# Segment attention with unpadded queries, products in quarter and half tiles of the array, and 16 products for the subtraction

## The chip, the cores and the metric

The kernel runs on one core of a Trainium2 chip, in a single launch over a batch of 64 sequences. The metric is the device time of that launch in microseconds (us). The kernel before took 1803.2 us (median of three runs, 1799.8 to 1804.67).

The engines are named as in the profile: PE is TensorE (matrix products, out of PSUM banks 2 KB wide), PEld its loading of the stationary operand, DVE is VectorE, ACT is ScalarE, POOL is GpSimd and SP issues the transfers. They run at once and wait for one another through semaphores.

## The reference, cut to what matters

Every sequence (128 positions, 128 features) goes through a cross-attention block and then this block, of which the change touches the scores and the softmax alone:

```python
xn = rms_norm(x, attn_norm_w)
q, k, v = split(xn @ to_qkv_w)          # 16 heads of 64
q, k = rope(q), rope(k)
kf = concatenate([k_extra, pm, k])      # 16 equal memory keys, 16 persistent keys, 128 own keys
vf = concatenate([v_extra, pm_v, v])
mask = (causal & same_segment) | (ki < 32)   # segments of 64 positions
scores = where(mask, einsum('bhid,bhjd->bhij', q, kf) * 64 ** -0.5, -1e30)
probs = softmax(scores)
o = einsum('bhij,bhjd->bhid', probs, vf)
x = x + o @ to_out_w
x = x + (silu(g) * a) @ ff_w2 + ff_b2        # a, g = halves of rms_norm(x) @ ff_w1 + ff_b1
```

A query sees only the 64 keys of its own segment and the memory keys. The 16 memory keys are equal, so one key with the weight 16 stands for them: 64 + 1 + 16 = 81 keys (`KEYS`) for each segment.

## The kernel before

**Stages and order.** Three sequences are in work at a time. `body(c, a, f)` holds for each engine the instructions of one round: the cross attention of sequence c, the segment attention of sequence a = c - 1 and the output projection and feed-forward of f = c - 2. The 64 sequences give 66 rounds, of which 62 hold all three. The order on each engine is the order of the code, written out by hand; engines meet only in semaphores. PSUM has eight banks: two for the cross attention, four for the segment attention, two for the feed-forward. A helper, `banks`, gives the tasks of a group its banks in turn, and a task may start only when the task before it in its bank has been read.

**The segment attention on PE.** Heads go in pairs, eight pairs of two heads. The transposed queries are copied by ACT into `qpad` (`turned`, L472, two copies of 64 partitions for each half of the pairs). In it the two heads of a pair and one segment form 128 columns; head 0 has its values in partitions 0 to 63 and zeros below, head 1 the other way round, so that one product with the pair's 128 rows of keys gives both heads' scores. Keys are in `kall` by pair and segment, 81 columns each, copied by DVE (L723).

The softmax needs the maximum of each query. It is taken from a first product in bf16 with queries as rows: for each of four tiles `max0` to `max3` one product that adds the causal mask (L979, 256 columns) and four with 81 columns (L982). DVE reduces each tile (L730) and writes the negated maxima as a bf16 pair, high part (L735) and rest (L739), into `mt`; each takes two instructions, for 64 partitions and 64 partitions. The scores proper are a second product in fp32 with keys as rows: 16 products of 128 columns (L872, `scores(t)`), four to a bank. Then PE turns the maxima (L990), ACT copies them into `shift_b`, and 32 products of 64 columns (L880, `less_maxima`) add maxima and mask to the scores. ACT takes the exponentials (L581, `probs`), PE weighs the values (L888, `weigh`), DVE divides (L675, L676, into `o`), and PE turns the result in the next round (L898).

**What stands around it.** In the same round PE does the cross attention's scores and its weighing (L854), which waits for ACT's exponentials (L523), which wait for DVE's clamping (L658). After L854 come the maxima (L979, L982), the scores (L872), L996 (the output projection of the cross attention, which waits for DVE's `c0T`, L668), L880, L1005 (the end of the feed-forward) and L888. The next round begins with L905, the transpose of `xn`: it waits for `xn` (DVE, L785) and for the bank that `pv1` had, which DVE frees with the second L676. DVE's order is: clamp, key copies (L723), a reciprocal (L662), the four maxima (L730), `mt`, a second reciprocal, `c0T`, `sT` (L752), the layer norm `r`, `bn`, `y` (L758 to L770) with a step on POOL in it (L464), then L675 and L676 with `xn` between. ACT's order is: the four L523, the second `turned`, the values `vall` (L472), `shift_b`, four `probs`. The fourth tile of the maxima waits for `vall`, as it takes the bank of the values.

## Time and profile before

| | |
|---|---|
| median of three runs | 1803.2 us |
| lowest and highest | 1799.8, 1804.67 us |
| span of the profiled execution, first to last instruction | 1801.7 us |
| mean granted TensorE clock | 0.997 of full speed |
| PE, PEld, DVE busy | 1666.4, 1434.9, 1543.8 us |
| ACT, POOL busy | 1073.9, 856.9 us |
| transfers from HBM | 21.46 MB read, 14 GB/s over the span with the writes |

The page gives no time for the profiled execution but its span. PE's records overlap, since a matmul's record reaches from its start to the end of its results; a busy PE is therefore not PE at its limit, and the distance from one start to the next is the figure to read. A product in fp32 leaves two records, each with its own load of weights; one in bf16 leaves one.

### The profile page before, as it was taken

What the parts mean: (1) busy time and instruction counts of PE and PEld (TensorE: products, weight loads), DVE (VectorE), ACT (ScalarE), POOL (GpSimd) and SP (SyncE); (2) the same over time, 40 slices, a digit from 0 to 9 for tenths busy, and PEclk for the clock granted to TensorE, in tenths of its full rate; (3) what the DMA queues carried; (4) which work ended last, traced back from release to release, by engine and by line L of the source; (5) the groups of instructions that cost most, each with busy time, mean ns of one, the idle gap of its engine ahead of it and who ended that gap; (6) DMA issues with size and microseconds to landing.
All of it is one profiled execution on the core that took longest, in us unless ns stands there. A gap on an engine that the chain in (4) does not pass through costs nothing.

```text
span 1801.7 us, 52360 instructions
## 1 busy us (share of the span) xinstructions
PE 1666.4 (92%) x17891; PEld 1434.9 (80%) x17891; DVE 1543.8 (86%) x3730; ACT 1073.9 (60%) x2637; POOL 856.9 (48%) x1107
## 2 busy tenths in 40 slices
PE   4899999999999999999999999999999999999997
PEld 3788788788888887888888888887888888878876
DVE  5788888889889889888888888888888898898894
ACT  3555656655656656656556556566566556566563
POOL 4344534535535535445445445445355355355352
PEclk9999999999999999999999999999999999999999
DMA  6000000000000000000000000000000000000000
GB/s 176 17 9 11 10 10 11 8 13 11 8 13 11 8 13 11 8 11 12 8 11 13 8 11 13 8 11 8 12 11 8 13 11 8 13 11 8 13 6 6
DMA packets 32411, 26.14 MB, mean 15 GB/s; under 512 B 8118, under 2 KB 31179, under 8 KB 32139
## 3 DMA queue, kind: packets, MB, share of 16 engines
q1 hardware_dynamic: 32394, 25.93, 5.4%
q8 instruction: 9, 0.15, 0.0%
q14 instruction: 8, 0.06, 0.0%
HBM read 21.46 MB, written 4.46 MB: 14 GB/s over the span
## 4 chain that ended last, share of the span: by engine, by line
DVE 49%; PE 22%; issue 21%; ACT 3%; POOL 3%; DVEq 1%; DMA 1%; SPq 0%; ACTq 0%; POOLq 0%
DVE z L658 9%; PE psum L927 6%; DVE ra L641 5%; DVE z L650 5%; DVE rb L644 5%; DVE mx L730 4%; PE psum L854 4%; DVE rden L662 3%; PE psum L898 3%; DVE sT L752 3%; DVE o L676 3%; DVE c0T L668 2%; ACT z L523 2%; POOL st L464 2%; DVE y L770 1%
## 5 line engine op out<-in xcount | busy, mean ns | idle before, releaser
L409 POOL TENSOR_TENSOR ra<-ra,rb 128x512 f32<-128x512 f32 x256 | 332.2, 1324 | 0.2
L464 POOL TENSOR_TENSOR st<-st,nhalf 128x1 f32<-128x1 f32 x64 | 38.3, 598 | 535.4 <-DVE st L763 535.4
L872 PE MATMUL psum<-qpad,kall 128*81 128x128 f32 x2048 | 251.6, 276 | 0.0
L641 DVE TENSOR_TENSOR ra<-psum,rope 128x512 f32<-128x512 f32 x256 | 174.3, 681 | 77.9 <-PE psum L838 77.8
L872 PEld LDWEIGHTS psum<-qpad,kall 128*81 128x81 f32 x2048 | 224.9, 151 | 2.6
L658 DVE TENSOR_SCALAR z<-z 77x512 f32<-77x512 f32 x256 | 216.8, 885 | 0.0
L581 ACT ACTIVATE probs<-psum 81x512 f32<-81x512 f32 x256 | 131.3, 593 | 142.3 <-PE psum L880 142.3
L523 ACT ACTIVATE z<-z 77x512 f32<-77x512 f32 x256 | 154.1, 627 | 67.1 <-DVE z L658 65.5
L854 PE MATMUL psum<-z,v 77*64 77x128 f32 x2048 | 141.6, 280 | 44.9 <-ACT z L523 44.9
L644 DVE TENSOR_TENSOR rb<-psum,rope 128x512 f32<-128x512 f32 x256 | 173.0, 676 | 0.0
L836 PE MATMUL psum<-wqkv_hi,xnT_hi 128*128 128x512 f32 x384 | 168.6, 439 | 2.7 <-DVE xnT_lo L681 1.8
L854 PEld LDWEIGHTS psum<-z,v 77*64 77x64 f32 x2048 | 112.5, 138 | 69.6 <-issue 68.6
L650 DVE TENSOR_TENSOR z<-psum,wT 77x512 f32<-77x512 f32 x256 | 163.1, 674 | 4.8 <-PE psum L846 4.8
L418 POOL TENSOR_TENSOR q0T_rest<-q0T,q0T_hi 128x128 f32<-128x128 f32 x64 | 29.3, 457 | 288.9 <-ACT k0T_hi L537 288.9
L472 ACT ACTIVATE qpad<-psum 64x512 f32<-64x512 f32 x256 | 151.9, 593 | 3.1
L472 ACT ACTIVATE vall<-psum 64x512 f32<-64x512 f32 x256 | 151.2, 591 | 3.1
L838 PE MATMUL psum<-wqkv_hi,xnT_lo 128*128 128x512 f32 x384 | 152.9, 398 | 0.0
L837 PE MATMUL psum<-wqkv_lo,xnT_hi 128*128 128x512 f32 x384 | 152.4, 397 | 0.0
L863 PE MATMUL psum<-cross_w,ra 128*128 128x128 f32 x1024 | 143.2, 273 | 0.1
L863 PEld LDWEIGHTS psum<-cross_w,ra 128*128 128x128 f32 x1024 | 122.2, 141 | 20.7 <-ACT vall L472 0.4
L888 PE MATMUL psum<-vall,probs 81*64 81x65 f32 x4096 | 133.6, 223 | 0.3 <-ACT probs L581 0.3
L888 PEld LDWEIGHTS psum<-vall,probs 81*64 81x64 f32 x4096 | 124.8, 137 | 8.0 <-issue 0.4
(141 smaller groups left out, 4028.3 us busy)
## 6 DMA issues: line engine op xcount, KB each, us to landing
seq_in<-in SPq DMA_DIRECT2D x64, 166.5 KB
out<-out_sb SPq DMA_DIRECT2D x64, 64.0 KB, 1.6
maskT<-in SPq DMA_DIRECT2D x64, 38.5 KB
vall<-memv_dram SPq DMA_DIRECT2D x128, 4.0 KB, 1.9
ctx_all<-in SPq DMA_DIRECT2D x5, 320.0 KB, 12.3
wqkv<-in SPq DMA_DIRECT2D x1, 1536.0 KB, 10.1
stage<-in SPq DMA_DIRECT2D x1, 1296.0 KB
ctx_all<-in SPq DMA_DIRECT2D x3, 288.0 KB, 11.3
```

Source lines behind the costliest of these rows:

```text
L409: nc.gpsimd.tensor_tensor(ra[:, sl], ra[:, sl], rb[:, sl], ALU.add).then_inc(rot_ready, 1)
L472: copy = lambda out, in_, **k: nc.scalar.activation(out, in_, ACT.Copy, **k)
L523: nc.scalar.activation(zt, zt, ACT.Exp, scale=float(HD0) ** -0.5).then_inc(exp0_ready, 1)
L641: V.tensor_tensor(ra[:, sl].rearrange("n (h d) -> n h d", h=8), p, rope[:, 0, :].unsqueeze(1).broadcast_to([S, 8, DH]), ALU.mult)
L644: V.tensor_tensor(rb[:, sl].rearrange("n (h e t) -> n h e t", h=8, t=2), p, rope[:, 1, :].rearrange("n (e t) -> n e t", t=2).unsqueeze(1). ...
L650: V.tensor_tensor(z0[:, 4 * t:4 * t + 4, :], cross_at(f"score{t}")[0:S2, :].rearrange("k (h q) -> k h q", h=4), wT[:].unsqueeze(1).broadca ...
L658: V.tensor_scalar(zt, zt, lim, -lim, ALU.min, ALU.max).then_inc(clip_ready, 1)
L836: mm(self_at(name), xnT_hi[:], wqkv_hi[:, w], stop=False)
L854: last = mm(cross_at(f"pv{t}")[half:half + 64, 0:S], v0_flat[:, lo:lo + 64], z0[:, 4 * g + r, :], start=r == 0, stop=r == 3)
L863: last = nc.tensor.transpose(self_at(f"{name}T")[:, 128 * n:128 * (n + 1)], ra[:, lo + 128 * n:lo + 128 * (n + 1)], ident[:])
L872: mm(self_at(f"score{t}")[0:KEYS, 128 * n:128 * (n + 1)], kall[:, pair, s, :], qpad[:, pair, s, :, :].rearrange("p h i -> p (h i)"), start ...
L888: last = mm(self_at(f"pv{t}")[SEG * s:SEG * (s + 1), VW * n:VW * (n + 1)], probs[:, pair, s, h, :], vall[s][:, w:w + VW])
```

## The change

Queries lose their zeros: `qT` holds each pair's 128 rows by 128 positions, and one ACT copy of 128 partitions takes the place of two of 64. Since a head's queries and keys lie in one half of the partitions, products run on half of the array's rows: head 0 of a pair in rows 0 to 63, head 1 in rows 64 to 127, each into a bank of its own. The tiles `t` now hold four heads of one parity in place of two pairs; a step works on two banks at a time (`maxima(half)`, `scores(half)`).

- Maxima: per half two mask products, then 16 products of 64 rows, 64 queries and 81 keys. Queries of segment 0 go to partitions 0 to 63 and of segment 1 to 64 to 127, so each product uses a quarter of the array.
- Negated maxima: `mt` has 128 partitions and 16 columns for each part; two DVE instructions in place of four.
- Scores: 32 fp32 products of 64 rows, 81 keys and 64 queries in place of 16 with 128 rows and 128 columns.
- Subtraction: 16 products of 128 columns in place of 32 of 64. The selecting table is half as large.
- The turned maxima go to the unused last 128 columns of the feed-forward's `gate` bank, with a semaphore of their own, and no longer through a bank of the segment attention.
- `o` is written with a stride of two heads; `turn_heads(t)` waits for two tiles at once.

```diff
-        qpad = sb("qpad", [128, PAIRS, NSEG, 2, SEG])
+        qT = sb("qT", [128, PAIRS, S])
...
-                    for h in range(2):
-                        rows = slice(DH * h, DH * (h + 1))
-                        last = copy(qpad[rows, 4 * t:4 * t + 4, :, h, :],
-                                    self_at(f"q{t}T")[rows, :].rearrange("p (c s i) -> p c s i", c=4, s=NSEG))
-                    last.then_inc(q_ready, 1)
+                    copy(qT[:, 4 * t:4 * t + 4, :].rearrange("p c i -> p (c i)"), self_at(f"q{t}T")).then_inc(q_ready, 1)
...
+                    then(V.tensor_scalar(mt[:, 0, :], mx[:], -1.0, None, ALU.mult), self_steps, "hi", a)
+                    V.scalar_tensor_tensor(out=mt[:, 1, :], in0=mx[:], scalar=-1.0, in1=mt[:, 0, :],
+                                           op0=ALU.mult, op1=ALU.subtract).then_inc(mt_ready, 1)
...
+                def maxima(half):
+                    if half == 1:
+                        wait(pe, self_free("max3", a))
+                    for t in (2 * half, 2 * half + 1):
+                        p = self_at(f"max{t}")[:, 0:4 * KEYS].rearrange("i (n k) -> i n k", n=4)
+                        mm(p[:, :, 0:SEG], ident_b[:], causal_b[:].unsqueeze(1).broadcast_to([128, 4, SEG]), stop=False)
                     for n in range(4):
+                        for h in range(2):
+                            t, dims = 2 * half + h, slice(DH * h, DH * (h + 1))
+                            for s in range(NSEG):
+                                queries = slice(SEG * s, SEG * (s + 1))
+                                last = mm(self_at(f"max{t}")[queries, KEYS * n:KEYS * (n + 1)], q_upper[dims, 4 * half + n, queries],
+                                          k_upper[dims, 4 * half + n, s, :], start=False)
+                            if n == 3:
+                                last.then_inc(self_fill(f"max{t}"), 1)
+
+                def scores(half):
+                    wait(pe, self_free(f"score{2 * half + 1}", a))
+                    for n in range(4):
+                        for s in range(NSEG):
+                            for h in range(2):
+                                t, dims = 2 * half + h, slice(DH * h, DH * (h + 1))
+                                mm(self_at(f"score{t}")[0:KEYS, S * n + SEG * s:S * n + SEG * (s + 1)], kall[dims, 4 * half + n, s, :],
+                                   qT[dims, 4 * half + n, SEG * s:SEG * (s + 1)], start=n == 0 and s == 0, stop=False)
 
                 def less_maxima(t):
                     for n in range(4):
-                        pair, s = 2 * t + n // 2, n % 2
-                        p = self_at(f"score{t}")[0:KEYS, 128 * n:128 * (n + 1)]
-                        for h in range(2):
-                            last = mm(p[:, SEG * h:SEG * (h + 1)], select_b[:, (2 * pair + h) * NSEG + s, :], shift_b[:], start=False)
+                        last = mm(self_at(f"score{t}")[0:KEYS, S * n:S * (n + 1)], select_b[:, 4 * t + n, :], shift_b[:], start=False)
...
+                    maxima(0)
+                    maxima(1)
                     scores(0)
+                    if f is not None:
+                        pe.wait_ge(gate_ready, f + 1)
+                    pe.wait_ge(mt_ready, a + 1)
+                    mm(shift_at[0:2 * H, :], mt[:].rearrange("i p h -> i (p h)"), ident_b[:]).then_inc(shift_filled, 1)
                     scores(1)
```

PE before, in the loop, from the cross attention's weighing (`z,v`) to the turned maxima (`stack_b,mt`); in brackets the semaphores waited for:

```order
L854 MATMUL psum<-z,v 64x128 x7
L972 REGISTER_ALU
L979 MATMUL psum<-causal_b,ident_b 128x4x64 [waits memk_ready,k_ready,q_ready]
L982 MATMUL psum<-kall,qpad 128x81 x4
L979 MATMUL psum<-causal_b,ident_b 128x4x64
L982 MATMUL psum<-kall,qpad 128x81 x4
...
L979 MATMUL psum<-causal_b,ident_b 128x4x64 [waits v_ready]
L982 MATMUL psum<-kall,qpad 128x81 x4
L872 MATMUL psum<-qpad,kall 81x128 [waits max_ready]
L872 MATMUL psum<-qpad,kall 81x128 x3
...
L990 MATMUL psum<-stack_b,mt 64x64 [waits mt_ready,max_ready]
```

The same stretch of PE in the changed kernel, to `cross_w,c0T` (L996 before):

```order
L844 MATMUL psum<-z,v 64x128 x7
L974 REGISTER_ALU
L862 MATMUL psum<-causal_b,ident_b 128x4x64 [waits memk_ready,k_ready,q_ready]
L862 MATMUL psum<-causal_b,ident_b 128x4x64
L868 MATMUL psum<-kall,qT 64x81 x16
L862 MATMUL psum<-causal_b,ident_b 128x4x64 [waits v_ready]
...
L879 MATMUL psum<-qT,kall 81x64 [waits max_ready]
L879 MATMUL psum<-qT,kall 81x64 x15
L983 MATMUL psum<-ident_b,mt 32x128 [waits mt_ready,gate_ready]
...
L987 REGISTER_ALU [waits shift_ready]
L988 MATMUL psum<-cross_w,c0T 128x128 [waits c0T_ready]
```

The first tile of the maxima was complete after one mask product and four others, and is now complete after two mask products and 14 small ones. The wait for `v_ready` stood before the fourth tile and stands now before the third and fourth.

DVE before, from the third and fourth maxima to the second reciprocal:

```order
L730 TENSOR_REDUCE mx<-psum 128x4 [waits self_bank4_filled]
L732 ISA
L735 TENSOR_SCALAR mt<-mx 64x16 [waits max_ready]
L735 TENSOR_SCALAR mt<-mx 64x16
L99 REGISTER_ALU
L739 SCALAR_TENSOR_TENSOR mt<-mx,mt 64x16 [waits self_step]
L739 SCALAR_TENSOR_TENSOR mt<-mx,mt 64x16
```

and in the changed kernel:

```order
L726 TENSOR_REDUCE mx<-psum 128x4 [waits self_bank4_filled]
L728 ISA
L729 TENSOR_SCALAR mt<-mx 128x16 [waits max_ready]
L99 REGISTER_ALU
L730 SCALAR_TENSOR_TENSOR mt<-mx,mt 128x16 [waits self_step]
```

Two of the four instructions are gone; the wait of the second part for the first has stayed.

## Rows read from the trace of the kernel before

**Rows 1.** The page: engines' busy time; shares of the chain that ended last.
```profile
PE 1666.4 (92%) x17891; PEld 1434.9 (80%) x17891; DVE 1543.8 (86%) x3730; ACT 1073.9 (60%) x2637; POOL 856.9 (48%) x1107
DVE 49%; PE 22%; issue 21%; ACT 3%; POOL 3%; DVEq 1%; DMA 1%; SPq 0%; ACTq 0%; POOLq 0%
```

**Rows 2.** The chain of waits, two rounds: start us, us, what.
```profile
906.25 1.09 PE psum L854 x16
...
910.39 0.97 DVE rden L662
...
917.72 0.32 PE psum L905
...
944.97 0.32 PE psum L905
```

**Rows 3.** The timeline of DVE: start us, us, what [idle before <-releaser].
```profile
907.87 1.72 DVE L730 TENSOR_REDUCE mx<-psum 128x4 f32<-128x324 f32 x4 [0.36 <-PE psum L982]
909.62 0.35 DVE L735 TENSOR_SCALAR mt<-mx 64x16 bf16<-64x16 f32 x2
911.38 1.20 DVE L668 TENSOR_TENSOR c0T<-psum,rden 32x128 f32<-32x128 f32 x4
912.61 0.86 DVE L752 SCALAR_TENSOR_TENSOR sT<-psum,cols,ug 128x128 f32<-128x128 f32 x3
...
908.68 0.90 DVE L730 TENSOR_REDUCE mx<-psum 128x4 f32<-128x324 f32 x2
```

**Rows 4.** Waits over the whole span: total us, times, longest.
```profile
PE psum L905 <- DVE o L676: 36.5, 63, 0.7
```

**Rows 5.** The timeline of PE in the same round.
```profile
907.50 0.33 PE L982 MATMUL psum<-kall,qpad 128*128 128x81 bf16 x4
908.60 0.29 PE L979 MATMUL psum<-causal_b,ident_b 128*128 128x256 bf16 x1 [0.23 <-ACT vall L472]
908.89 1.94 PE L872 MATMUL psum<-qpad,kall 128*81 128x128 f32 x16
910.76 0.22 PE L990 MATMUL psum<-stack_b,mt 128*64 128x64 bf16 x1
...
912.72 0.40 PE L996 MATMUL psum<-cross_w,c0T 128*128 128x128 f32 x2
912.95 1.42 PE L880 MATMUL psum<-shift_b,select_b 128*81 128x64 bf16 x32
...
915.05 2.09 PE L888 MATMUL psum<-vall,probs 81*64 81x65 f32 x64
```

**Rows 6.** Groups of PE instructions, shapes apart: count, busy us, mean ns.
```profile
L872 PE MATMUL psum<-qpad,kall 128*81 128x128 f32 x2048 | 251.6, 276 | 0.0
L854 PE MATMUL psum<-z,v 77*64 77x128 f32 x2048 | 141.6, 280 | 44.9 <-ACT z L523 44.9
L888 PE MATMUL psum<-vall,probs 81*64 81x65 f32 x4096 | 133.6, 223 | 0.3 <-ACT probs L581 0.3
L880 PE MATMUL psum<-shift_b,select_b 128*81 128x64 bf16 x2048 | 90.8, 203 | 0.0
```

**Rows 7.** The timeline of PE, the last two transposes before L854, and L854.
```profile
904.17 0.38 PE L863 MATMUL psum<-cross_w,ra 128*128 128x128 f32 x2
...
904.48 1.09 PE L854 MATMUL psum<-z,v 77*64 77x128 f32 x16
```

**Rows 8.** The timeline of ACT in the same round; one group of ACT (mean ns).
```profile
906.13 1.20 ACT L472 ACTIVATE qpad<-psum 64x512 f32<-64x512 f32 x2
907.35 1.20 ACT L472 ACTIVATE vall<-psum 64x512 f32<-64x512 f32 x2
...
L472 ACT ACTIVATE oT<-psum 128x512 f32<-128x512 f32 x128 | 76.6, 599 | 36.2 <-PE psum L898 31.4
```

**Rows 9.** First round with segment attention (DVE), and the last one (PE).
```profile
66.35 0.29 DVE L758 TENSOR_TENSOR r<-psum,xb 128x128 f32<-128x128 f32 x1 [0.58 <-PE psum L996]
...
1777.11 1.94 PE L872 MATMUL psum<-qpad,kall 128*81 128x128 f32 x16
```

More of the change, by code:

```diff
@@ L146, in build @@
         causal_b = sb("causal_b", [128, SEG], BF16)
-        select_b = sb("select_b", [128, H * NSEG, KEYS], BF16)
-        stack_b = sb("stack_b", [128, SEG], BF16)
-        shift_b = sb("shift_b", [128, SEG], BF16)
+        select_b = sb("select_b", [128, H, KEYS], BF16)
+        shift_b = sb("shift_b", [128, S], BF16)
         seq_in = sb("seq_in", [128, S + S2 + D])
@@ L392, in _ @@
             nc.gpsimd.memset(nhalf[:], -0.5).then_inc(nhalf_set, 1)
-            for t in (v0, *vall, qpad, mt, half_gate, tanh_gate):
+            for t in (v0, *vall, half_gate, tanh_gate):
                 nc.gpsimd.memset(t[:], 0.0).then_inc(zeros_step, 1)
-            pool.wait_ge(zeros_step, 7)
+            pool.wait_ge(zeros_step, 5)
             nc.gpsimd.memset(v0[:, :, :, 4 * HD0:5 * HD0], 1.0).then_inc(zeros_set, 1)
@@ L576, in body @@
                     values(1)
-                    wait(act, self_filled("shift", a))
-                    copy(shift_b[0:64, :], self_at("shift")[0:64, 0:SEG]).then_inc(shift_ready, 1)
+                    act.wait_ge(shift_filled, a + 1)
+                    copy(shift_b[0:2 * H, :], shift_at[0:2 * H, :]).then_inc(shift_ready, 1)
                     for t in range(4):
                         wait(act, self_filled(f"score{t}", a))
-                        nc.scalar.activation(probs[:, 2 * t:2 * t + 2, :, :, :].rearrange("k c s h i -> k (c s h i)"),
+                        nc.scalar.activation(probs[:, 4 * t:4 * t + 4, :].rearrange("k n i -> k (n i)"),
                                              self_at(f"score{t}")[0:KEYS, :], ACT.Exp, scale=float(DH) ** -0.5).then_inc(probs_ready, 1)
@@ L732, in body @@
                     dve.wait_ge(max_ready, a * 4 + 4)
-                    for h in range(2):
-                        rows = slice(SEG * h, SEG * (h + 1))
-                        last = V.tensor_scalar(mt[rows, h, 0, :], mx[rows, :], -1.0, None, ALU.mult)
-                    then(last, self_steps, "hi", a)
-                    for h in range(2):
-                        rows = slice(SEG * h, SEG * (h + 1))
-                        last = V.scalar_tensor_tensor(out=mt[rows, h, 1, :], in0=mx[rows, :], scalar=-1.0, in1=mt[rows, h, 0, :],
-                                                      op0=ALU.mult, op1=ALU.subtract)
-                    last.then_inc(mt_ready, 1)
+                    then(V.tensor_scalar(mt[:, 0, :], mx[:], -1.0, None, ALU.mult), self_steps, "hi", a)
+                    V.scalar_tensor_tensor(out=mt[:, 1, :], in0=mx[:], scalar=-1.0, in1=mt[:, 0, :],
+                                           op0=ALU.mult, op1=ALU.subtract).then_inc(mt_ready, 1)
                 if c is not None:
@@ L1032, in constants @@
     i = np.arange(SEG)
+    stack = np.tile(np.eye(SEG), (2, 1)).astype(f)
     causal = np.tile(np.where(i[None, :] > i[:, None], NEG, 0.0), (2, 1)).astype(f)
-    stack = np.tile(np.eye(SEG), (2, 1)).astype(f)
-    shift = np.concatenate([np.zeros((64, SEG)), np.where(i[:, None] > i[None, :], NEG, 0.0)]).astype(f)
-    select = np.zeros((128, H, NSEG, KEYS), f)
-    for s in range(NSEG):
-        for part in range(2):
-            for h in range(H):
-                select[h % 2 * 32 + part * 16 + h // 2 * NSEG + s, h, s, :] = 1.0
+    shift = np.tile(np.concatenate([np.zeros((64, SEG)), np.where(i[:, None] > i[None, :], NEG, 0.0)]), (1, NSEG)).astype(f)
+    select = np.zeros((128, H, KEYS), f)
+    for part in range(2):
+        for h in range(H):
+            select[part * H + h, h, :] = 1.0
     for j in range(SEG):
-        select[64 + j, :, :, j] = 1.0
+        select[64 + j, :, j] = 1.0
     return {"ident": np.eye(128, dtype=f), "headmask": headmask, "rope": rope,
```

57 lines of the change are left out of this document (17 added, 40 removed).

## The prediction

> **What bounds the kernel now.** I read the engines' busy time first. PE stands at 92% and DVE at 86% [rows 1], and that alone doesn't say which of them to relieve. The shares of the chain that ended last do: DVE holds 49% of it, PE 22% [rows 1]. So I followed the chain of waits through one round. From the start of L905 at 917.72 to the next at 944.97 it is 27.25 us [rows 2], and 62 rounds of this form make up most of the span. In it PE has the chain in two places. One is the stretch from L905 to the output projection, which the change leaves alone. The other is L854, from 906.25, and behind it the first tile of the maxima [rows 2], which the change rewrites. From the first L730 on, at 907.87 after an idle time of 0.36 us on DVE [rows 3], the chain is DVE's, but for a step on POOL, until L905. There it is PE that waits: for `o` of DVE, 63 times, 36.5 us in all, 0.58 us a round [rows 4].
>
> The reader is to see in this that most of what PE saves behind the maxima, the scores and the subtraction, lies beside DVE's chain. It makes PE's wait at L905 longer and the round no shorter. What counts is when the four maxima are reduced, and how long `mt` takes. I therefore work out one moment: the start of the second reciprocal L662, at 910.39 before [rows 2].
>
> **Spacing of products.** Records overlap, so I take the distance between starts: length of a series less one record, over the number of gaps. Full array, fp32, 128 columns (L872): (1.94 - 0.276)/15 = 0.111 us a record [rows 5, 6]. Half the array's columns, fp32, 128 columns, two halves in turn (L854): (1.09 - 0.28)/15 = 0.054 [rows 6, 7]. Same columns, half the distance: two column halves do run at once. With 65 columns (L888) it is (2.09 - 0.223)/63 = 0.030 [rows 5, 6]. In bf16 on the full array, 64 columns (L880) take (1.42 - 0.203)/31 = 0.039 and 81 columns (L982) (0.33 - 0.20)/3 = 0.042 [rows 5, 6].
>
> **Change of tile form.** The last transpose L863 starts at 904.17 + 0.38 - 0.27 = 904.28; the next start is due 0.111 later, at 904.39, and L854, on half the columns, starts at 904.48 [rows 7]: 0.09 late. The same at L990, narrower than what stands around it: due at 908.89 + 16 x 0.111 = 910.67, started at 910.76 [rows 5], 0.09 again. Each change of form costs 0.09. The Trainium skill (TensorEngine Tiling (Array Packing), Key Properties) says that changing the tiling mode, not just the tile, drains TensorE; the trace agrees with its 0.09 us. It speaks against this change, which alternates between full and quarter tiles.
>
> **ACT's copies.** `turned` costs 1.20 us from 906.13 [rows 8] and becomes one copy of 128 partitions by the same 512 columns: 0.60, as each of the two now takes, since a copy of 128 partitions (`oT`, 599 ns [rows 8]) takes no longer than one of 64. So `q_ready` comes at 906.73 in place of 907.33, and `vall` ends at 907.95 in place of 908.55. The last L854 starts at 906.25 + 1.09 - 0.28 = 907.07 [rows 2, 6]; the next start is due at 907.13 and, after a change of form, at 907.22. Before, L979 came at 907.38, 0.12 ahead of L982 at 907.50 [rows 5]. Gain here: 0.16. What is late next is PE itself.
>
> **Maxima, first half.** Two L979 take 2 x 0.12 = 0.24, then 0.09 for the form: the first small product starts at 907.55. The last one of tile 0 is the fourteenth, 13 distances on. No row shows products on half of the rows, so the distance X is bounded: from above 0.042 us (L982, nothing overlaps), from below 0.042/4 = 0.010 (all four quarters at once). I take 0.030, the shortest that any row has (L888), and it is from products that overlap in just this manner; by columns alone two at once would need 0.021, but L880 shows by 0.039 for 64 columns that small products don't shrink with their columns. Tile 0 then has its last start at 907.94. Before, the last L982 started at 907.50 + 0.33 - 0.20 = 907.63 and L730 at 907.87, 0.24 later. Now L730: 908.18, later by 0.31.
>
> **Second half.** PE is free at 907.55 + 16 x 0.030 = 908.03 and with a change of form at 908.12, after `vall` (907.95, and 0.05 to wake PE, as 908.55 to 908.60 before [rows 5, 8]). So the wait that moved ahead of two tiles costs nothing here. Then 0.24 + 0.09 + 0.39 + 0.24: tile 2 can be reduced at 909.08. DVE would be there at 908.18 + 0.81 (the third L730 stood at 908.68, 0.81 behind the first [rows 3]) = 908.99, so it waits 0.09. From the third L730 to `mt` it was 909.62 - 908.68 = 0.94 [rows 3]: now 910.02, later by 0.40.
>
> **`mt`.** Before 910.39 - 909.62 = 0.77. The second of each two costs about 0.18 (0.35 for two [rows 3], one 0.17). Two such go: 0.41 stay. L662 starts at 910.43, against 910.39: +0.04, or +0.03 with L888's unrounded 0.0297. Over 62 rounds +2 us.
>
> **The rest of PE.** Scores: 64 records in place of 32. With 64 columns and half of the rows I bound them by 0.030 (L888) and 0.057 (half of L872's 0.111, nothing overlaps), and take 0.039, since the 81 columns of weights are those of L880. That is 2.5 us in place of 3.6. Subtraction: 16 x about 0.058 = 0.9 in place of 32 x 0.039 = 1.25. All of it is covered: the second half of the scores ends near 911.9, L996 must wait for `c0T` (911.38 + 1.20 = 912.58 [rows 3]), and DVE needs L996 only after `sT`, at 913.39 or so. Even at 0.057 the scores end near 913.0 and L996 near 913.4, as DVE asks for it. Behind the new wait for `mt_ready` and `gate_ready` stands the second half of the scores, for which nobody waits before that; `gate_ready` is from several microseconds before. The turned maxima's own bank, the smaller `shift_b`, the coarser wait in `turn_heads` (L905 waits for the same second tile already) and the stride of `o` I cost at nothing, covered by the same wait of PE at L905 (0.58).
>
> **Ends.** In the first round with segment attention DVE waits 0.58 for L996 [rows 9] and `mt` is quicker: about -0.7. In the last round nothing of cross attention stands beside PE, which runs unbroken from 1777.11 [rows 9]; scores and subtraction count there, less the slower maxima and the wait for `mt`: about -0.9. The smaller table and the zeros no longer set lie beside loads in the setup.
>
> **Sum.** Span 1801.7 + 2 - 1.6 = 1802.1 us. The page gives no time around the span; the median of the runs stands 1.5 above it, inside their own spread, and I add it: 1803.6. What can be told from no change is 0.3%, 5.4 us.
>
> **Rivals.**
> Quarters overlap further (X at most 0.025). For it speaks that L854 shows full overlap of two halves, and that four quarters can be distinct here; against it that no row is under 0.030. At 0.025: L730 at 907.55 + 0.33 + 0.24 = 908.12, tile 2 at 908.94, `mt` at 909.88, L662 at 910.29, -0.10 a round: -6.5 - 1.6, that is 1795. At 0.010 the second half waits for `vall` at 908.00 and reduces at 908.70, so DVE binds: L730 at 907.92, L662 at 910.08, -0.31 a round: 1782. The Trainium skill gives such a floor (TensorEngine Tiling (Array Packing), Instruction Overhead): a matmul has about 60 cycles of overhead, so that one column takes as long as 60. By that rule X would be an estimated 0.025, this rival's 1795; no run here shows it yet.
>
> Half of the rows don't overlap (slower). X is that of the bf16 products on the full array, 0.0395. For it: rows in halves appear nowhere in the trace, and L880 and L982 are both near 0.04. L730 comes at 908.30, tile 2 at 907.55 + 0.63 + 0.09 + 0.24 + 0.09 + 0.51 + 0.24 = 909.35, L662 at 910.70: +0.32 a round, +20 - 1.6: 1821. It decides from X = 0.033 on: L662 moves by 29 X - 0.83, which is then 0.12 a round.
>
> PE becomes the bound: a load of weights into a half of the rows can't overlap with that half's product, the scores' distance is 0.030 + 0.057 = 0.087, 2.8 us for each half. From 909.1 on they end at 914.9 with the turned maxima between, L996 ends 2.0 us after DVE asks for it, and a round is 2.0 longer: 1925. Against it: L888 alternates in the same manner and shows none of this.
>
> **Chances.** Forecast 0.44, its own range 1799 to 1809 (X from 0.027 to 0.033). More overlap 0.29, no overlap 0.23, PE as the bound 0.04. A tenth of the forecast falls below -0.3% and as much above +0.3%. Faster: 0.29 less a twentieth, and 0.05: 0.33. Slower: 0.23 + 0.04 + 0.04: 0.31. Same: 0.36. The range takes in 0.010 us on one side and 0.042 on the other: 1781 to 1824.
>
> **What would show it.** The distance between starts in the small products of the maxima, 0.030; L730's first start 1.93 us behind that of the last L854 group (before 1.62), its idle time 0.6 to 0.7 in place of 0.36; 0.41 from the first `mt` to L662; idle time of PE at L905 about 1.2 and a new one of some 0.6 before L996, with the round at 27.28. A round shorter by 0.1 or more, or an idle time of DVE before the third L730 over 0.3, would make the prediction wrong.

## The result, and the profile after

The changed kernel takes 1790.68 us (median of four runs, 1787.09 to 1794.01) against 1801.85 for the kernel before, measured beside it (four runs, 1799.8 to 1804.67). The ratio is 0.9933 with an interval of 0.9913 to 0.9952: faster by 0.7%. No change was forecast, so the forecast was wrong; the rival "Quarters overlap further" had the mechanism. Ratios, here and below, are those on record, taken only over executions within 1.5% of the fastest of their kernel (this leaves out one of e7); they are not the quotient of the two medians.

| profiled execution | before | after |
|---|---|---|
| its time, us | not given | 1787.09 |
| span, us | 1801.7 | 1785.3 |
| mean granted TensorE clock | 0.997 | 0.995 |
| 62 full rounds, start to start of the transpose of `xn` | 55 of about 27.24, 6 of 27.54, 1 of 28.48 | 29 of about 26.87, 32 of 27.17, 1 of 29.93 |
| before the second transpose of `xn`; from the last one to the end | 70.64; 39.33 | 69.00; 37.87 |

The spans differ by 16.4 us. The base round, the shortest common one, is 0.37 shorter, 62 x 0.37 = 22.9 us gained. 26 more rounds are 0.30 longer (+7.8), the one round in which the clock falls costs 3.06 in place of 1.24 (+1.8), and the two ends are 1.6 and 1.5 shorter. -22.9 + 7.8 + 1.8 - 3.1 = -16.4.

The page after, against [rows 1]: busy time, and the shares of the chain that ended last.

```profile
PE 1579.7 (88%) x19939; PEld 1321.2 (74%) x19939; DVE 1524.4 (85%) x3601; ACT 985.5 (55%) x2509; POOL 852.2 (48%) x1105
DVE 50%; PE 23%; issue 20%; POOL 3%; ACT 3%; DVEq 1%; DMA 1%; SPq 0%; ACTq 0%; POOLq 0%
```

PE has lost 87 us of busy time and the chain is DVE's as before. The waits over the whole span (total us, times, longest), against [rows 4]:

```profile
PE psum L907 <- DVE o L672: 60.0, 63, 1.0
PE psum L988 <- DVE c0T L664: 32.0, 63, 2.3
```

PE waits 23.5 us more at the start of a round, and there is a new wait for `c0T`: what PE saved behind the maxima turned into waiting, as was argued. A third wait was in no forecast: before the scores PE now waits for DVE to read the first maxima, 23.5 us in all (L879 below). The gain has to be in front of the second reciprocal. PE's timeline in a round with the clock at 1.00 (start us, us, what), against [rows 5, 7]:

```profile
922.77 1.09 PE L844 MATMUL psum<-z,v 77*64 77x128 f32 x16 [1.01 <-ACT z L520]
923.79 0.40 PE L862 MATMUL psum<-causal_b,ident_b 128*128 128x256 bf16 x2
924.12 0.35 PE L868 MATMUL psum<-kall,qT 64*64 64x81 bf16 x16
924.41 0.40 PE L862 MATMUL psum<-causal_b,ident_b 128*128 128x256 bf16 x2
924.73 0.35 PE L868 MATMUL psum<-kall,qT 64*64 64x81 bf16 x16
925.46 1.38 PE L879 MATMUL psum<-qT,kall 64*81 64x64 f32 x32 [0.38 <-DVE mx L726]
...
928.78 0.49 PE L988 MATMUL psum<-cross_w,c0T 128*128 128x128 f32 x2 [0.48 <-DVE c0T L664]
929.10 1.06 PE L884 MATMUL psum<-shift_b,select_b 128*81 128x128 bf16 x16
...
933.87 0.32 PE L907 MATMUL psum<-cross_w,xn 128*128 128x128 f32 x1 [0.97 <-DVE o L672]
```

and the groups that give one record's length (busy us, mean ns), against [rows 6]:

```profile
L879 PE MATMUL psum<-qT,kall 64*81 64x64 f32 x4096 | 178.2, 237 | 23.6 <-DVE mx L726 23.5
L868 PE MATMUL psum<-kall,qT 64*64 64x81 bf16 x2048 | 45.7, 209 | 0.0
```

The distance between starts of the small maxima products is (0.35 - 0.209)/15 = 0.009 us, not 0.030. (The timeline merges records; by the starts of the single ones it is 0.155/15 = 0.010.) That of the scores is (1.38 - 0.237)/31 = 0.037; I had taken 0.039. DVE's timeline in the same round, against [rows 2, 3]:

```profile
924.51 1.70 DVE L726 TENSOR_REDUCE mx<-psum 128x4 f32<-128x324 f32 x4 [0.49 <-PE psum L868]
926.24 0.17 DVE L729 TENSOR_SCALAR mt<-mx 128x16 bf16<-128x16 f32 x1
926.45 0.17 DVE L730 SCALAR_TENSOR_TENSOR mt<-mx,mt 128x16 bf16<-128x16 f32 x1
926.54 0.95 DVE L658 RECIPROCAL rden<-psum 128x128 f32<-128x128 f32 x1
```

The four maxima run on without a gap, and the second reciprocal starts 3.77 us behind the start of L844. Before it was 910.39 - 906.25 = 4.14 [rows 2]. The difference is the 0.37 of the base round. Its parts, before and after: from the start of the weighing to the first maximum 1.62 and 1.74, from there to `mt` 1.75 and 1.73, from `mt` to the reciprocal 0.77 and 0.30. Against the kernel before, the gain is thus all in `mt`.

The longer rounds come from DVE's clamps. Here are the clamps of the second pair and POOL beside them, first in a base round and then in a long one:

```profile
893.22 1.29 POOL L446 TENSOR_TENSOR ug<-ug,half_gate 128x384 f32<-128x384 f32 x1
893.24 1.55 DVE L654 TENSOR_SCALAR z<-z 77x512 f32<-77x512 f32 x2
...
920.09 0.99 POOL L446 TENSOR_TENSOR ug<-ug,half_gate 128x384 f32<-128x384 f32 x1
920.11 1.85 DVE L654 TENSOR_SCALAR z<-z 77x512 f32<-77x512 f32 x2
```

The pair takes 1.55 or 1.85 us, and when it takes 1.55 it is POOL's multiplication that is lengthened, 1.29 in place of 0.99. Both kernels have both forms, and in these two traces the changed one has the dear one more often. Whether the two engines hold each other up there is what e2 tests.

### The profile page after: what moved, and what is told of

It is laid out like the page before. It is cut to its first block, busy times and chain, and to the rows that moved or that the text cites. A ratio compares the mean times of both kernels' runs of the same rounds, so it can differ in the third digit from the quotient of the medians.

```text
span 1785.3 us, 55646 instructions
## 1 busy us (share of the span) xinstructions
PE 1579.7 (88%) x19939; PEld 1321.2 (74%) x19939; DVE 1524.4 (85%) x3601; ACT 985.5 (55%) x2509; POOL 852.2 (48%) x1105
## 4 chain that ended last, share of the span: by engine, by line
DVE 50%; PE 23%; issue 20%; POOL 3%; ACT 3%; DVEq 1%; DMA 1%; SPq 0%; ACTq 0%; POOLq 0%
DVE z L654 8%; PE psum L929 6%; DVE ra L637 5%; DVE z L646 5%; DVE rb L640 5%; DVE mx L726 4%; PE psum L844 4%; DVE rden L658 3%; PE psum L900 3%; DVE sT L742 3%; DVE o L672 3%; DVE c0T L664 2%; ACT z L520 2%; POOL st L465 2%; DVE x1sq L688 2%
## 5 line engine op out<-in xcount | busy, mean ns | idle before, releaser
L410 POOL TENSOR_TENSOR ra<-ra,rb 128x512 f32<-128x512 f32 x256 | 332.3, 1328 | 0.2
L654 DVE TENSOR_SCALAR z<-z 77x512 f32<-77x512 f32 x256 | 225.5, 919 | 0.0
L520 ACT ACTIVATE z<-z 77x512 f32<-77x512 f32 x256 | 161.1, 636 | 114.6 <-DVE z L654 108.1
L879 PE MATMUL psum<-qT,kall 64*81 64x64 f32 x4096 | 178.2, 237 | 23.6 <-DVE mx L726 23.5
L844 PE MATMUL psum<-z,v 77*64 77x128 f32 x2048 | 141.5, 280 | 55.3 <-ACT z L520 55.3
L879 PEld LDWEIGHTS psum<-qT,kall 64*81 64x81 f32 x4096 | 160.4, 150 | 36.2 <-DVE mx L726 31.9
L844 PEld LDWEIGHTS psum<-z,v 77*64 77x64 f32 x2048 | 112.5, 138 | 80.1 <-issue 78.1
L726 DVE TENSOR_REDUCE mx<-psum 128x4 f32<-128x324 f32 x256 | 108.8, 487 | 31.9 <-PE psum L868 31.8
```

Source lines behind the costliest of these rows:

```text
L410: nc.gpsimd.tensor_tensor(ra[:, sl], ra[:, sl], rb[:, sl], ALU.add).then_inc(rot_ready, 1)
L520: nc.scalar.activation(zt, zt, ACT.Exp, scale=float(HD0) ** -0.5).then_inc(exp0_ready, 1)
L654: V.tensor_scalar(zt, zt, lim, -lim, ALU.min, ALU.max).then_inc(clip_ready, 1)
L726: V.reduce_max(mx[:, 4 * t:4 * t + 4], self_at(f"max{t}")[:, 0:4 * KEYS].rearrange("i (n k) -> i n k", n=4), AX_X).then_inc(max_ready, 1)
L844: last = mm(cross_at(f"pv{t}")[half:half + 64, 0:S], v0_flat[:, lo:lo + 64], z0[:, 4 * g + r, :], start=r == 0, stop=r == 3)
L879: mm(self_at(f"score{t}")[0:KEYS, S * n + SEG * s:S * n + SEG * (s + 1)], kall[dims, 4 * half + n, s, :], qT[dims, 4 * half + n, SEG * s:S ...
```

## The experiments

Each kernel is the changed one with the edit shown, unless another is named. "Base round" is the shortest common distance between two transposes of `xn`. The kernel before, run beside them, had medians of 1800.75, 1803.78 and 1801.74 in the three groups of runs (e1 to e4, e5 to e8, e9 to e11).

**e1: `mt` in four instructions.**

```diff
-                    then(V.tensor_scalar(mt[:, 0, :], mx[:], -1.0, None, ALU.mult), self_steps, "hi", a)
+                    for h in range(2):
+                        rows = slice(SEG * h, SEG * (h + 1))
+                        last = V.tensor_scalar(mt[rows, 0, :], mx[rows, :], -1.0, None, ALU.mult)
+                    then(last, self_steps, "hi", a)
...
```

> The changed kernel with the negated maxima again in two instructions of 64 partitions for each part, four in all. If the fewer instructions for mt are what shortens a round, then from the first mt instruction to the second reciprocal it is 0.77 us again in place of 0.30, a round has 27.34 us in place of 26.87, and 62 rounds cost 29 us: about 1820 us. The forecast's own figure for this step was 0.36 us a round: about 1813 us. Rival: the gain comes from the products and the copies alone; then the time stays at 1791 us, within 5.

Measured: 1817.68 (1813.21 to 1827.9), ratio to before 1.0079 (1.0052 to 1.0107). DVE's timeline:

```profile
923.12 0.35 DVE L731 TENSOR_SCALAR mt<-mx 64x16 bf16<-64x16 f32 x2
923.51 0.35 DVE L735 SCALAR_TENSOR_TENSOR mt<-mx,mt 64x16 bf16<-64x16 f32 x2
923.90 0.96 DVE L658 RECIPROCAL rden<-psum 128x128 f32<-128x128 f32 x1
```

From `mt` to the reciprocal it is 0.78, against 0.30 with two instructions, and the base round is 27.35, 0.48 longer. Two tiny instructions are worth their full 0.24 us each on this chain.

**e2: POOL's multiplications of `ug` held back until the last clamp.**

```diff
+                    if c is not None:
+                        pool.wait_ge(clip_ready, c * 4 + 4)
```

> The changed kernel, in which POOL starts its two products for the feed-forward's gate (ug) only when DVE has done the last of the four clamps (one more wait on POOL, in rounds with cross attention). Theory: the rounds of 27.17 us beside those of 26.87 come from the third and fourth clamp (SBUF to SBUF, one source) running at the same time as POOL's ug, and DVE and POOL can't both use what they share: whichever comes second stands still. Then the pair of clamps takes about 0.75 us in place of 1.55 or 1.85, all rounds get one length near 26.1 us, and the time is 1735 to 1745 us. Rival: the long rounds come from something else (ACT's exponentials beside the clamps, PE's clock); then both lengths stay and the time stays within 10 us of 1791, or gets longer because ug is late for DVE's sT.

Measured: 1739.53 (1737.56 to 1740.78), ratio 0.9656 (0.9638 to 0.9674). DVE and POOL:

```profile
923.62 0.75 DVE L656 TENSOR_SCALAR z<-z 77x512 f32<-77x512 f32 x2
...
924.45 1.00 POOL L446 TENSOR_TENSOR ug<-tanh_gate,half_gate 128x384 f32<-128x384 f32 x1 [1.88 <-DVE z L656]
```

(This L446 is the first multiplication, with `tanh_gate`, which stands in L444 of the changed kernel.) The pair takes 0.75, 61 of the 62 rounds are 26.24 to 26.28 long (one 26.17), and no round has a fall of the clock. So the two engines do hold each other up, and both the 0.30 of the long rounds and another 0.6 of every round came from it. The first pair of clamps still takes 1.85 in every round here, beside POOL's `ra` (L410); that one was not held back in any run. The Trainium skill (SBUF — State Buffer, Who interferes with whom) states that VectorE in a two-port mode and GpSimd share a port pair, one of them waiting for the whole instruction of the other. The runs agree: 0.75 alone, 1.55 or 1.85 beside POOL. They don't show the port itself, and the order of the starts doesn't tell who gets it: in all 62 rounds of the changed kernel POOL's multiplication starts first. Where the clamp follows 0.012 to 0.024 us behind, the first clamp runs undisturbed (0.41) and the second takes 1.22; where it follows 0.022 to 0.025 behind, the first takes 1.26 and POOL is not lengthened.

**e3: the small maxima products four in a row on one quarter** (head outermost, then segment, then pair).

```diff
-                    for n in range(4):
-                        for h in range(2):
-                            t, dims = 2 * half + h, slice(DH * h, DH * (h + 1))
-                            for s in range(NSEG):
+                    for h in range(2):
+                        t, dims = 2 * half + h, slice(DH * h, DH * (h + 1))
+                        for s, n in [(s, n) for s in range(NSEG) for n in range(4)]:
...
```

> The changed kernel with the 16 small products of a half in another order: four in a row use the same quarter of the array (first the head, then the segment, then the pair), so that no two neighbours lie in different quarters except at three places. If the distance of 0.009 us between them comes from four quarters at work at once, it grows to 0.035 to 0.042 us, the first tile of the maxima comes about 0.15 us later, the third one 0.5 us later, and a round is about 0.3 us longer: 1805 to 1812 us. If the small products are quick for another reason (64 rows, no drain between them), the distance stays near 0.01 and the time at 1791 us.

Measured: 1783.46 (1780.43 to 1788.14), ratio 0.9906 (0.9883 to 0.993). PE's timeline:

```profile
921.84 0.38 PE L867 MATMUL psum<-kall,qT 64*64 64x81 bf16 x16
```

The distance is (0.38 - 0.209)/15 = 0.011, the base round 26.90. The time is below that of the changed kernel since 11 rounds are long and not 32, and none has a fall of the clock. My expectation missed: products need not take turns among quarters to overlap, at least with four in a row. That left two readings, which e7 tells apart.

**e4: the queries turned in two copies of 64 partitions.**

```diff
-                    copy(qT[:, 4 * t:4 * t + 4, :].rearrange("p c i -> p (c i)"), self_at(f"q{t}T")).then_inc(q_ready, 1)
+                    for h in range(2):
+                        rows = slice(DH * h, DH * (h + 1))
+                        last = copy(qT[rows, 4 * t:4 * t + 4, :].rearrange("p c i -> p (c i)"), self_at(f"q{t}T")[rows, :])
+                    last.then_inc(q_ready, 1)
```

> The changed kernel with ACT's copy of the turned queries in two instructions of 64 partitions each, as before. By the timeline the values (vall) then end 0.6 us later, and with them the second half of the maxima starts about 0.4 us later, so that DVE waits 0.2 us before the third maxima: a round of 27.07 us in place of 26.87, +12 us, 1803 us. If ACT's copy is covered by PE and DVE (rival), the time stays at 1791 us. How many rounds have the longer pair of clamps may change too, as ACT's instructions move; a theory in which only DVE and POOL decide it expects about half of them again.

Measured: 1815.77 (1813.91 to 1823.37), ratio 1.0091 (1.006 to 1.0121); base round 27.40, 0.53 longer. PE and DVE:

```profile
909.64 1.09 PE L847 MATMUL psum<-z,v 77*64 77x128 f32 x16 [0.72 <-ACT z L523]
910.77 0.40 PE L865 MATMUL psum<-causal_b,ident_b 128*128 128x256 bf16 x2
...
911.48 0.90 DVE L729 TENSOR_REDUCE mx<-psum 128x4 f32<-128x324 f32 x2 [0.59 <-PE psum L871]
911.99 0.40 PE L865 MATMUL psum<-causal_b,ident_b 128*128 128x256 bf16 x2 [0.54 <-ACT vall L473]
...
912.70 0.90 DVE L729 TENSOR_REDUCE mx<-psum 128x4 f32<-128x324 f32 x2 [0.32 <-PE psum L871]
913.63 0.17 DVE L732 TENSOR_SCALAR mt<-mx 128x16 bf16<-128x16 f32 x1
```

The first maximum comes 0.10 later (1.84 behind the start of the cross attention's weighing in place of 1.74), and the first maximum to `mt` takes 2.15 in place of 1.73: PE now waits for `vall` before the second half of the maxima. The copy saved there is worth more than the 0.16 that I gave it, since without it the wait that was moved ahead of two tiles binds.

**e5: the kernel before, with e2's wait.**

> The kernel before, with POOL's two multiplications of ug held back until the last clamp of z is done, as in the run of the changed kernel with the same wait. Theory A (the clamps lose to POOL's neighbouring work in both kernels alike, and apart from it the change is worth its shorter maxima and mt, 0.37 us a round): the second pair of clamps falls from 1.55 to 0.75 us, all rounds have one length near 26.6, the time is 1755 to 1765, and the changed kernel with the wait (1739.5) stands 0.985 to 0.991 to it. Rival B (part of the change's gain was a different phase of the same collision): rounds of 26.3 to 26.4, 1740 to 1747, and the two kernels with the wait stand within 0.3% of each other.

Measured: 1762.66 (1760.1 to 1765.63), ratio 0.9764 (0.9746 to 0.9781); 61 rounds of about 26.60 and one of 26.53. The changed kernel with the same wait (e2) has 26.26: 0.34 a round, 62 x 0.34 = 21 us, and its ratio to before over this one's is 0.9656/0.9764 = 0.989. So with the clamps undisturbed the change is worth 1.1%, and 0.34 to 0.37 a round is its own in either surrounding.

**e6: the scores with 8 products (16 records) in a row on one half of the rows.** A half of the scores has 16 products, which leave 32 records; the expectation below calls them 32 products.

```diff
-                    for n in range(4):
-                        for s in range(NSEG):
-                            for h in range(2):
+                    for h in range(2):
+                        for n in range(4):
+                            for s in range(NSEG):
```

> The changed kernel with the 32 score products of a half ordered by head first, so that 8 in a row use the same rows of the array and write the same bank, where before two row halves took turns. Theory (the scores lie beside DVE's chain, as the prediction has it): whatever the distance becomes, up to 0.06 us, the round stays at 26.87 and the time within 0.5% of the changed kernel, 1782 to 1798; PE waits less for c0T. Rival (PE is the bound there): each half of the scores grows from 1.4 to about 2.0 us and the round by 0.3 or more, over 1805.

Measured: 1996.45 (1988.66 to 2009.64), ratio 1.107 (1.1015 to 1.1126), mean granted clock 0.896. A round with the clock at 1.00 throughout (28.0 long):

```profile
1578.69 2.29 PE L879 MATMUL psum<-qT,kall 64*81 64x64 f32 x32 [0.37 <-DVE mx L726]
1580.91 0.23 PE L983 MATMUL psum<-ident_b,mt 128*32 128x128 bf16 x1
1581.07 2.29 PE L879 MATMUL psum<-qT,kall 64*81 64x64 f32 x32
...
1583.29 0.49 PE L988 MATMUL psum<-cross_w,c0T 128*128 128x128 f32 x2
...
1583.82 0.29 DVE L748 TENSOR_TENSOR r<-psum,xb 128x128 f32<-128x128 f32 x1 [0.98 <-PE psum L988]
```

The distance is (2.29 - 0.237)/31 = 0.066, almost twice 0.037: with the halves taking turns two products really run side by side. The single records start 0.073 apart within one half of the rows, here and in the changed kernel, and the other half's first one starts at 1579.61, when the first half has three records left to start. DVE waits 0.98 for L988, and the base round is 27.94, 1.07 longer, 66 us. The other 140 us or so are 53 rounds of 30.5 and more in which the clock falls. The windows of such a round (PE busy, PEld, DVE, ACT, POOL with counts; granted clock, share and rate of transfers):

```profile
910.00:912.50 2.50, 2.35 (x33) 2.25 (x33) 2.39 (x7) 0.00 (x0) 0.00 (x0) 1.00 0.00 0
912.50:914.00 1.50, 1.50 (x19) 1.47 (x19) 1.42 (x6) 0.27 (x1) 0.00 (x0) 0.73 0.00 0
914.00:916.00 2.00, 2.00 (x19) 1.92 (x17) 0.31 (x2) 0.00 (x0) 0.00 (x0) 0.50 0.00 0
```

From 2.4 GHz the clock goes to 1.2 GHz in the midst of the scores, between 912.50 and 914.00, with PE busy 2.35 of the 2.50 us before. My theory, no change, was wrong, and the rival was right in kind and far too small. The prediction had said that up to 0.057 the scores stay covered; 0.066 is past that.

**e7: one quarter of the array with 16 small products, the others with 4.** Twelve products more, into unused columns.

```diff
+                                if h == 0 and s == 0 and half == 0 and n < 3:
+                                    for extra in range(4):
+                                        mm(self_at(f"max{t}")[queries, KEYS * 4:KEYS * 5], q_upper[dims, 4 * half + n, queries],
+                                           k_upper[dims, 4 * half + n, s, :], start=False)
```

> The changed kernel with 12 more of the small maxima products before the first tile is complete: each of head 0, segment 0 and the first three pairs is repeated four times into unused columns of the same bank, so that one quarter of the array has 16 products and the others 4. Theory A (each quarter works through its own products beside the others, a product taking the time of its 81 columns, 0.034 us, so the distance of 0.009 seen is four at once): the 28 products take at least 16 x 0.034 = 0.54 us from first to last start where 16 took 0.14, the first L726 comes 0.35 to 0.45 later behind L844, and the time rises by 0.3 to 0.4 us a round, to 1807 to 1817. Rival B (such a product is short by itself wherever it goes, 0.009 to 0.012 us): 28 take 0.25 to 0.34, the first L726 comes 0.12 to 0.2 later, and the time is 1795 to 1803. Rival C (a product on the same quarter as the last one costs the full 0.037 to 0.042 that products cost on the whole array): 12 x 0.04 + 16 x 0.009 = 0.62, later by 0.5, 1820.

Measured: 1844.32 (1819.11 to 1850.97), ratio 1.0152 (1.0068 to 1.0236). L868 are the old products, L872 the added ones:

```profile
904.57 0.22 PE L868 MATMUL psum<-kall,qT 64*64 64x81 bf16 x1
...
904.79 0.20 PE L868 MATMUL psum<-kall,qT 64*64 64x81 bf16 x1
...
904.99 0.20 PE L868 MATMUL psum<-kall,qT 64*64 64x81 bf16 x1
...
905.18 0.20 PE L868 MATMUL psum<-kall,qT 64*64 64x81 bf16 x1
...
905.42 1.70 DVE L726 TENSOR_REDUCE mx<-psum 128x4 f32<-128x324 f32 x4 [0.95 <-PE psum L868]
```

28 products take 0.61 us from first to last start. Five on the loaded quarter take 0.19 to 0.22, and 0.61/15 = 0.041 for each of its 16. The other twelve cost nothing visible. Theory A holds in its form (B's 0.34 is ruled out) with 0.041 in place of 0.034 for a product: what 81 columns take on the full array too, 0.042 (L982 in [rows 5]). C's 0.62 fits this run as well as A does, but not e3, where C's rule makes 12 x 0.04 + 3 x 0.009 = 0.51 us of the 0.17 measured. The same number accounts for most of the changed kernel and e3: four products a quarter are 3 x 0.041 = 0.12 us from first to last start, against 0.155 and 0.184 by the single records.

The single records show two things more. In each group the three other products start when the loaded quarter has three of the products before them left to start; products thus start out of their order, by up to three places a quarter here. Their ends are told in order all the same: the product that signals the first tile, last in the order, ended at 905.29, but L726 starts at 905.42, behind the end of the loaded quarter's last one, at 905.37. DVE's idle time rises from 0.49 to 0.95, and the base round by the same 0.46, to 27.33: up to here a delay of the first maximum counts in full. The rest of the lost time is 12 rounds of 30.4 with a fall of the clock. The Trainium skill (TensorEngine Tiling (Array Packing), Key Properties) says that different tiles can load and multiply in parallel; 0.009 and 0.041 agree. Its Instruction Overhead, some 60 cycles a matmul, holds at most within a tile: 0.009 is far below the estimated 0.025.

**e8: the changed kernel again.**

> The changed kernel once more, unchanged, on this chip. Theory (the length of a round, 26.87 or 27.17, depends on where the clamps meet POOL's multiplications, and with it the number of long rounds is set by the kernel's timing): again 25 to 40 of 62 rounds are long and the rest 26.87, and the time is 1787 to 1794. Rival (which rounds are long is chance or the chip's): the number is under 15 or over 50, and the time moves by 0.3 us for each.

Measured: 1782.51 (1779.68 to 1784.67), ratio 0.9873 (0.9857 to 0.9889). 40 rounds of about 26.87, one of 27.09, 20 of 27.17, one with a fall of the clock. Neither expectation holds: the number of long rounds is not fixed by the kernel. 12 fewer long rounds are 3.6 us; the two profiled executions differ by 2.4 (1787.09 and 1784.67). The medians differ by 8.2. In the first measurement the other executions had mean clocks of 0.987 to 0.993, here of 0.991 to 0.996; the trace of those executions isn't there, so the rest stays unexplained.

**e9: e1 and e4 together.**

> The changed kernel with both small edits undone together: the queries turned in two copies of 64 partitions, and mt in four instructions. What remains of the change is PE's work and the tile form. Theory (the change's gain lies in these two edits, and the rest of it costs): the two losses add up, 0.48 + 0.53 = 1.0 us a round, rounds of 27.85 to 27.95 and 1843 to 1860, well above the kernel before; the rest of the change by itself then costs 0.6 us a round. Rival (the two overlap, one hides behind the other): rounds of 27.4 to 27.6 and 1815 to 1830, and the rest of the change costs 0.3 or less.

Measured: 1873.95 (1868.78 to 1890.82), ratio 1.0391 (1.0357 to 1.0426), clock 0.934 in the profiled execution. The base round is 27.86, which is 0.99 more: 0.48 + 0.53 add up. The time is above the range I gave, since 32 rounds are 28.6 or longer with falls of the clock. In rounds with the clock at 1.00 what remains of the change (tile form, fewer and smaller products, order) costs 27.86 - 27.24 = 0.62 against the kernel before: 0.22 at the first maximum, which now needs two mask products, and 0.40 between it and `mt`, where the second half waits for `vall`.

**e10: the scores in runs of four products on one half of the rows.**

```diff
-                    for n in range(4):
+                    for h, n in [(h, n) for pairs in ((0, 1), (2, 3)) for h in range(2) for n in pairs]:
                         for s in range(NSEG):
-                            for h in range(2):
+                            if True:
```

> The changed kernel with the 32 score products of a half in runs of 4 products (8 records) on the same half of the rows, then 4 on the other half. With a change of half at every product the distance between records was 0.037 us, with 16 products in a row 0.066, and four small maxima products in a row on one quarter still overlapped. Theory (products on different parts of the array overlap as long as the next one on another part is not far behind in the order; 4 is within reach): 0.037 to 0.042, no change of the time, 1780 to 1795. Rival (the overlap needs the two halves to alternate at each product in fp32): 0.06 or more, rounds of about 27.9 with clock losses on top, 1900 or more.

Measured: 1791.11 (1788.35 to 1798.06), ratio 0.9952 (0.9931 to 0.9973). PE's timeline:

```profile
927.38 1.82 PE L879 MATMUL psum<-qT,kall 64*81 64x64 f32 x32 [0.38 <-DVE mx L726]
929.13 0.23 PE L983 MATMUL psum<-ident_b,mt 128*32 128x128 bf16 x1
929.29 1.82 PE L879 MATMUL psum<-qT,kall 64*81 64x64 f32 x32
```

The distance is (1.82 - 0.237)/31 = 0.051, between 0.037 and 0.066 and outside both expectations: the overlap is half lost with four in a row. Time and base round (27.00, +0.13) are near the theory's, as the cover of the scores ends just there. So the order in which parts of the array are used matters for the fp32 scores, at four in a row already, and not for four bf16 ones. That need not lie in the type: four fp32 products are eight records and four bf16 ones are four, and here again the other half's first record (927.72) starts when three of the eight (927.79, 927.86, 927.93) are left. Longer runs of bf16 products were not tried.

**e11: e2 and e3 together.**

> The two edits together that each made the changed kernel no slower: POOL's multiplications of ug held back until the last clamp, and the small maxima products ordered four in a row on one quarter, head 0 first. Theory (with the collision gone all rounds have one length, 26.26, and the order of the small products moves the first maximum by at most 0.03 us): 1736 to 1743, the same as with the first edit alone. Rival (head 0 first completes the first tile earlier, after 8 of 16 products, by 0.06 us or more a round): 1733 to 1737.

Measured: 1740.25 (1738.31 to 1743.6), ratio 0.9658 (0.9636 to 0.968), rounds of 26.28. The same as e2, as the theory has it. e2 remains the fastest version: 3.4% below the kernel before.

## Why the prediction was wrong

**What bounds the kernel: right.** PE's saving behind the maxima became waiting, in the round shown 0.97 us at L907 (forecast 1.2), 0.48 at L988 (0.6) and 0.38 at L879, which was not forecast. The one moment to work out was the second reciprocal. It was forecast at 4.18 us behind the start of the weighing and came at 3.77. The 0.41 fall on three terms, the first of which is the failed step.

**X, the distance of the small products: mis-sized.** Taken 0.030, measured 0.009. From the first small product to the reduction I had 13 x 0.030 + 0.24 = 0.63; it took 924.51 - 924.12 = 0.39, 0.24 less. The first mask product came 1.02 behind L844 in place of 0.97, so the first maximum came 0.19 early: 1.74 and not 1.93. The error was to take the shortest distance of any row. L888's 0.030 is from two column halves taking turns. I had the right lower bound, 0.042/4 = 0.010, and argued against it that small products don't shrink with their columns. They don't: e7 shows 0.041 for each. But four quarters do them side by side, so the price is divided by the number of quarters and not by the size of the product.

**The third tile: follows from X.** I let DVE wait 0.09 before it. With the second half complete in time there was no wait, and the first maximum to `mt` took 1.73 in place of 1.84: 0.11.

**`mt`: mis-sized.** 0.77 became 0.30, not 0.41: 0.11 more. I took away the second instruction of each pair at 0.18. In e1 each pair takes 0.39 to the next start (923.12, 923.51, 923.90); with single instructions it is 0.21 and then only 0.09 (926.24, 926.45, 926.54): the reciprocal starts before the record of the last one ends (926.62). In e1 it starts 0.20 behind the start of the last one; why it is sooner with one instruction isn't shown. e1 shows the whole, 0.48.

**ACT's copy: right in place, too small in worth.** 0.16 was the gain at the start of the maxima. e4 shows 0.10 there and 0.42 more before `mt`, because `vall` would be late. The sentence that the moved wait costs nothing was right, and only thanks to this copy. e1, e4 and e9 together say where the gain is: two copies and two tiny instructions fewer give 1.0 us a round, and the rest of the change takes 0.6 of it back. The 0.42 that the copies save before `mt` is a wait that the change itself had moved ahead of the third tile, so they win nothing there against the kernel before. What two instructions for `mt` would give in the kernel before was not run.

**The scores: right, their cover too wide.** 0.037 measured, 0.039 taken, and covered. The cover was to reach to 0.057, but at 0.051 e10 loses 0.13 a round already: DVE asks for L988 0.37 earlier than I had it. e6 and e10 show how near the cover's end is, and that the 0.037 rests on the alternation of heads in the innermost loop.

**The change of form: near.** 924.12 - 923.79 = 0.33 for two mask products and the change, as 0.24 + 0.09.

**Ends.** Forecast -1.6, measured -3.1 for both.

**What no step had: clamps and clock.** I cost DVE's clamps at their old durations. They depend on POOL's work beside them, and long rounds went from 6 to 32 in the profiled executions, 7.8 us of loss that hid a third of the gain (e8, with 20, lost half of that). Rows 3 to 9 could not have told it, but the two forms of a clamp pair stood in the trace of before. Without this loss the rival's 1782 would have been nearly met: its X of 0.010 and its 0.31 a round stand against 0.009 and 0.37. Part of that is luck: it had the first maximum at 1.67, 0.07 too early, and `mt` at 0.41, 0.11 too long.

**Still open.** Why the number of long rounds differs between executions of one kernel (32 and 20) isn't shown: the two forms of the pair differ by hundredths of a microsecond in the distance of the starts (under e2), and what shifts them was not found. Nor is it shown what brings the clock down. Rounds with a fall are 1 of 62 in the kernel before, the changed one and e8, none in e2, e3, e5 and e11, 2 in e10, 3 in e4, 5 in e1, 12 in e7, 32 in e9 and 53 in e6. More work of PE alone does not order them: in e9 the rounds without a fall have more idle time of PE than in the changed kernel, 3.4 us against 2.5.

## What to carry to other kernels

Where products are to share the array, count for each part of the array its own products at the price that such a product has alone, and take the largest of these sums, here 4 x 0.041 us for 16 products (an estimate that is low by some 0.03). This held with at most five records in a row on one part. Order the long fp32 series so that neighbours use different parts. On a chain of DVE, count instructions before elements: halving four instructions with 16 columns gave 0.48 us a round and copies of 128 partitions in place of twice 64 on ACT 0.53 (most of it by removing a wait of the changed order), while the rest of the change cost 0.6. And look at every DVE instruction of which the trace has two or three durations: what POOL does beside it is the first thing to test, here worth more than the change itself.

## What the runs showed that I had not expected

- A small bf16 product (64 rows, 64 columns of weights, 81 columns) costs 0.041 us within its quarter of the array (e7), where products start out of their order but are told of in order, and sixteen over four quarters cost 0.14 to 0.17 us in either order (the changed kernel, e3).
- fp32 products on row halves (64 rows, 81 columns of weights, 64 columns): 0.037 us a record when the halves alternate at each product, 0.051 in runs of four products, 0.066 in runs of eight (e6, e10). In both runs a record on the other part starts when three of the part before are left to start.
- Two DVE clamps take 0.75 us alone and 1.55 or 1.85 beside POOL's multiplications (e2); which form comes up goes with a few thousandths of a microsecond between the starts.
- More work of PE can cost through the clock as well: in e6, 0.91 us more in each half of the scores made the base round 1.07 longer, and in 53 of 62 rounds the clock fell to 1.2 GHz and took 2.5 us or more besides.
